# Grouped attention in one pipelined loop: the output product behind the second projection, other fixed banks, and VectorE's row of work re-ordered

## The reference, cut to what matters

```python
ln_out = _ln(hidden_states, ln_w, ln_b)
q = _ln(fp8_linear(ln_out, wq), ...)      # 8 groups x 2 heads x 128
k = _ln(fp8_linear(ln_out, wk), ...)      # 8 groups x 128
v = fp8_linear(ln_out, wv)
core = gqa(q, k, v)                       # softmax attention within the sequence
qx = _ln(fp8_linear(ln_out, wqx), ...)
kx, vx = split(cond @ w_kv_x)             # keys and values from a context
xout = gqa(qx, _ln(kx), vx)
catq = div_clamp_fp8(concat(core, xout), proj_smooth)
x = x + (catq @ wproj) * scale
```

## Time and profile before

| | |
|---|---|
| median of 3 runs | 1064.17 us (1063.57 to 1068.45) |
| the profiled execution | 1067.66 us, its span 1066.0 us |
| PE busy | 920.6 us, 86% |
| DVE busy | 728.0 us, 68% |
| ACT busy | 566.9 us, 53% |
| POOL busy | 147.2 us, 14% |
| scores of slot 4 begin | 407.89 us |
| scores of slot 32 begin | 899.07 us |

### The profile page before, as it was taken

One profiled execution on the slowest core, in us unless ns is written; L12 is line 12 of the kernel. 1 busy time (PEld: TensorE's weight loads), 2 busy tenths in 40 slices (PEclk: granted clock), 3 DMA queues, 4 the chain that ended last, 5 costly groups with the idle time before them and its releaser, 6 DMA issues. The chain is left out here.

```text
span 1066.0 us, 15923 instructions
## 1 busy us (share of the span) xinstructions
PE 920.6 (86%) x5254; PEld 691.2 (65%) x5254; DVE 728.0 (68%) x1575; ACT 566.9 (53%) x2102; POOL 147.2 (14%) x190
## 2 busy tenths in 40 slices
PE   6989896999856589999999999999999987659597
PEld 3657664566545477778787887787877775444354
DVE  4564545567774777878787888787878786446554
ACT  4351333544524577777677777777777665121131
POOL 2001202000033411121212111111111120000000
PEclk9998998999888699999999999999999998769899
DMA  6010000000100042332332423324222522200000
GB/s 203 1 59 1 0 1 1 2 1 1 41 1 20 1 114 73 89 94 68 100 80 56 124 58 101 83 58 109 71 70 55 179 57 68 49 1 1 20 0 20
DMA packets 64081, 56.77 MB, mean 53 GB/s; under 512 B 11201, under 2 KB 62978, under 8 KB 64002
## 3 DMA queue, kind: packets, MB, share of 16 engines
q1 hardware_dynamic: 63904, 55.76, 19.7%
q10 hardware_dynamic: 98, 0.03, 0.0%
HBM read 21.15 MB, written 1.05 MB: 21 GB/s over the span
## 5 line engine op out<-in xcount | busy, mean ns | idle before, releaser
L1161 ACT ACTIVATE group_probs<-ps,score_bias 128x256 f32<-128x256 f32 x256 | 117.4, 484 | 57.0 <-DVE score_bias L1496 57.0
L837 PE MATMUL ps<-group_w_hi,xq 128*128 128x256 f32 (+1 forms) x512 | 131.1, 297 | 18.8 <-POOL xq L1704 11.6
L1118 ACT ACTIVATE group_squares<-ps 128x128 f32<-128x128 f32 x384 | 103.8, 297 | 71.9 <-PE ps L837 61.7
L1496 DVE TENSOR_REDUCE score_bias<-ps 128x2 f32<-128x512 f32 x128 | 88.1, 691 | 67.8 <-PE ps L891 67.8
L837 PE MATMUL ps<-group_w_lo,xq 128*128 128x256 f32 (+1 forms) x512 | 123.9, 283 | 0.0
L878 PE MATMUL ps<-group_probsT,group_values 128*128 128x512 f32 x256 | 117.3, 602 | 2.7 <-issue 2.7
L891 PE MATMUL ps<-group_kT,group_qT 128*128 128x256 f32 x512 | 115.8, 379 | 2.3 <-ACT group_qT L1127 2.3
L891 PEld LDWEIGHTS ps<-group_kT,group_qT 128*128 128x128 f32 x512 | 97.1, 190 | 28.4 <-issue 16.8
L837 PEld LDWEIGHTS ps<-group_w_hi,xq 128*128 128x128 f32 x512 | 100.2, 196 | 21.4 <-DVE group_heads L1482 7.6
L906 PE MATMUL ps<-group_wp_hi,group_cat 128*128 128x256 f32 x256 | 71.3, 312 | 43.0 <-DVE group_cat L199 43.0
L837 PEld LDWEIGHTS ps<-group_w_lo,xq 128*128 128x128 f32 x512 | 100.6, 196 | 0.8
(11 more groups left out here) (262 smaller groups left out, 1797.9 us busy)
## 6 DMA issues: line engine op xcount, KB each, us to landing
group_probsT<-second SPq DMA_DIRECT2D x512, 64.0 KB, 2.0
group_raw_p<-in_L_xattn_wproj_dram SPq DMA_DIRECT2D x16, 256.0 KB, 3.3
group_raw_w<-in_L_xattn_wq_dram SPq DMA_DIRECT2D x8, 256.0 KB, 3.1
group_raw_w<-in_L_xattn_wqx_dram SPq DMA_DIRECT2D x8, 256.0 KB, 3.1
group_raw_w<-in_L_xattn_w_kv_x_dram SPq DMA_DIRECT2D x16, 128.0 KB, 3.2
x_all<-in_x_dram SPq DMA_DIRECT2D x2, 512.0 KB, 5.9
front_work<-in_ctx_dram SPq DMA_DIRECT2D x1, 1024.0 KB, 6.8
group_raw_w<-in_L_xattn_wk_dram SPq DMA_DIRECT2D x8, 128.0 KB, 3.0
```

What stands on the lines that cost most here:

```text
L837: last = pe.matmul(c.ps[:, bank, at:at + width], x_, w[:, k, col:col + width], start=k == 0 and m == 0, stop=k == KD - 1 and m == 1)
L1118: act.activation(c.squares[:, t, 3 * i + h, :], c.ps[:, bank, h * HD:(h + 1) * HD], ACT.Square, accum_out=c.head_sum[:, t, 3 * i + h:3 * i ...
L1161: last = act.activation(c.probs[:, side, h, t, :], c.ps[:, fills.bank(name), t * S:(t + 1) * S], ACT.Exp, bias=c.score_bias[:, i:i + 1], a ...
L1496: v.tensor_reduce(c.score_bias[:, i:i + 2], c.ps[:, bank, :].rearrange("p (t n) -> p t n", n=S), AX.X, ALU.max, negate=True).then_inc(nega ...
```

## The change

The whole diff follows. On PE the output product of item n-4 comes behind the second projection of item n. The fixed banks of the fills become a plain turn of 5, 6, 4, 7. In slot 1 two transposes of tokens go to banks 4 and 7. On DVE the first side is laid before the second side's sums are inverted and before the weights; the second side is laid before the output product is added.

```diff
-FILL_BANKS = (5, 6, 4, 7, 4, 5, 6, 7, 4, 5, 6, 7)
+FILL_BANKS = (5, 6, 4, 7, 5, 6, 4, 7, 5, 6, 4, 7)
...
     if o.weights:
         fill(WEIGHTS, WEIGHTS + 1)
-    if o.outputs:
-        fill(ADD)
     if o.projects:
         f.plan(2, ("proj", o.n, 2))
         f.plan(3, ("proj", o.n, 3))
+    if o.outputs:
+        fill(ADD)
     if o.scores:
         fill(*range(HEADS_T, HEADS_T + 3))
     if o.n == 1:
-        f.plan(5, ("xT", "Q", 1, 0))
-        f.plan(6, ("xT", "Q", 1, 1))
+        f.plan(4, ("xT", "Q", 1, 0))
+        f.plan(7, ("xT", "Q", 1, 1))
...
                     if o.weights:
                         next_weights(o)
+                    if o.projects:
+                        project_item(o, 1)
                     if o.outputs:
                         output_item(o)
-                    if o.projects:
-                        project_item(o, 1)
                     if o.scores:
                         turn_item_heads(o)
...
                     if o.outputs:
                         quantise_item(o)
                     if o.turns:
+                        lay_item_probs(o, 0)
                         invert_sums(o, 1)
                     if o.weights:
                         next_weights(o)
                     if o.turns:
-                        lay_item_probs(o, 0)
+                        lay_item_probs(o, 1)
                     if o.outputs:
                         add_item(o)
-                    if o.turns:
-                        lay_item_probs(o, 1)
                     if o.projects:
                         normalise_item(o)
```

## The result

| | before | changed |
|---|---|---|
| median | 1066.53 us, 5 runs | 1075.44 us, 5 runs |
| ratio | | 1.0086, 95% interval 1.0047 to 1.0124 |
| span of the profiled execution | 1066.0 us | 1071.8 us |
| scores of slot 4 begin | 407.89 | 407.18 |
| scores of slot 32 begin | 899.07 | 907.23 |

A forecast was written before the change was run, and what follows sets the result against it. A loop through DVE and the output product bounds the kernel; afterwards averages wait for DVE's addition. Slots 4 to 31 give +6.4 us, with start and end +5.4, so the median becomes 1069.6 us (+0.51%), range 1062 to 1076.

The forecast's parts named there:

- The loop before: Old kernel's slots: a loop of scores, DVE, output product, second projection, heads and averages sets 17.55 us, whatever PE has to do.
- The averages behind the addition: PE's averages take bank 4 behind ADD, so they wait 0.5 to 1.5 us per slot for DVE's later addition; chance 0.55.
- The lengths: New slot is 16.85 us plus weights: 18.14, 18.53, 17.86 and 16.96 for types 0 to 3, against 17.56.
- the sum: Slots 4 to 31 together +6.4 us; with start and end +5.4 us.
- Other waits: New order's waits for product, weights and reciprocal are hidden; DMAs of `probs_laid` have just enough room, so nothing is added.
- The room of 13.18: Time in us from the second side's transpose to the next first one, for 16 DMAs; one observed case took 13.05.
- The loop through `probs_laid`: Second loop, through 16 DMAs; as rival bound it needs more than 13.18 us, up to +10 us, 1080; chance 0.07.
- POOL and DVE: Second side's multiplications on DVE fall beside POOL's root of 1.3 us; price on DVE nil.
- the rival: POOL and DVE lock each other out: the root's 1.3 in each of 28 slots, 36 us, 1106; chance 0.03.
- The start: Slot 1: ACT's wait of 0.81 us for a transpose behind bank 5 goes, -0.8 us.
- so I give it no chance of its own: Rival that PE's clock falls in the new idle, waits up to 1.5 us; no separate chance given.
- The tail: Slots 32 to 35: earlier laid sides against averages waiting for the addition, taken as equal, -0.2 us, up to 2 either way.

The follow-up runs named there:

- run 114: Not a label of a run: in "In the whole run 114 multiplications" the number counts DVE multiplications beside work of POOL in the changed kernel.

## Why the prediction was right, point by point

**The loop before.** Right. In the runs in which the product moved (with new banks; it was never moved alone) and the addition wasn't late, the slots are of PE's length.

**The averages behind the addition.** Right, and shown from both sides: freeing the bank alone, and the old DVE order alone, each take the loss away. PE waits there 0.7 to 1.7 us and not 0.5 to 1.5, since the claim comes free up to 0.09 later in three of the types and PE gets there some 0.1 earlier.

**The lengths.** Forecast 18.14, 18.53, 17.86 and 16.96, measured 18.28, 18.53, 18.00 and 17.11. The terms that were off are two: the release of the claim took 0.15 (619.28 to 619.43) and not 0.05, and from the start of the averages to the scores went 3.50 (619.43 to 622.93) and not 3.44. In type 1 the weights were done in 1.55 (633.28 to 634.83 in DVE's timeline) instead of 1.68, since ACT's part had ended 1.4 earlier (at 631.92), where before the two overlapped (626.69 in the earlier trace rows, ACT's part up to 627.55); that hid both. The slots 5 to 32 grew by 8.9 (500.05 less 491.18), where the sum for the same slots was 5.8: about 0.15 more in each but type 1. The direction hung on little: 0.2 us less in each slot would have been no change, as the prediction says, and the errors of the small terms happened to lie on the slower side.

**Other waits.** Right: in the changed kernel DVE doesn't wait for DMAs between 408 and 850 us, nor the addition for the product. The room of 13.18 held; it is 13.35 in the timeline (618.71 to 632.06). The loop through `probs_laid` was rightly named as next, and the run with the addition ahead of the second side hit it.

**POOL and DVE.** Right: the second side's multiplications, 616.30 for 1.13, ran into POOL's root, which starts at 617.04 in its timeline, and were not held. In the whole run 114 multiplications lie beside work of POOL, and all took 0.34 to 0.36. By the sentence of the Trainium skill (SBUF — State Buffer, "SBUF: two separate sides") an instruction of VectorE in a two-port mode would have been held for the whole of POOL's. In which mode the multiplications run no trace shows, so they don't speak against the sentence. Another instruction shows a hold, in both kernels: a step of the rounding that makes `xq`, of the same form as the step of L196 (0.43 throughout), here in timelines of slot 1 of the kernel before.

```profile
347.78 0.43 DVE L1448 TENSOR_SCALAR front_work<-front_work 128x1024 uint16<-128x1024 uint16 x1
349.77 2.22 DVE L1448 TENSOR_SCALAR front_work<-front_work 128x1024 uint16<-128x1024 uint16 x1
```

```profile
349.48 2.23 POOL L1704 TENSOR_TENSOR xq<-front_work 128x1024 fp32r<-128x1024 bf16 x1 [6.43 <-DVE front_work L1450]
```

Of its eight executions the three without POOL took 0.43 and the five beside POOL's product 2.22. The one shown ends 0.28 behind POOL's (351.99 against 351.71), as the sentence has it. So the rival had a real ground; rows 9 settled it for the multiplications, and would not have for every instruction of VectorE.

**The start.** Here the prediction was wrong about the clock: "so I give it no chance of its own". It had the slots in mind, and there the clock did stay at 1.00. The forecast gain in slot 1 came: ACT's wait of 0.81 is gone, and from slot 1's projection to the scores of slot 2 the changed kernel is 1.2 faster. But PE's wait ahead of those scores grew from 2.29 to 3.24, both times for ACT's copies of the turned heads. In the changed kernel the first of them starts 0.47 behind the end of PE's heads (368.86 against 368.39), before it started 0.35 ahead of it. Behind the longer wait the clock was low. Timelines of PE, before and changed:

```profile
374.51 3.69 PE L891 MATMUL ps<-group_kT,group_qT 128*128 128x256 f32 x16 [2.29 <-ACT group_qT L1127]
```

```profile
371.63 6.64 PE L891 MATMUL ps<-group_kT,group_qT 128*128 128x256 f32 x16 [3.24 <-ACT group_qT L1127]
```

The same 16 matmuls took 2.95 more, and the way from these scores to the next grew by as much, from 14.32 to 17.27. In windows of PE (length, busy, clock) the changed kernel has 0.50 there, the level of 1.2 GHz, and the kernel before 1.00:

```profile
371.60:375.00 3.40, 3.37 (x8) 0.50 0.41 99
```

```profile
374.50:378.30 3.80, 3.79 (x19) 1.00 0.42 101
```

Slot 4 then was 0.8 shorter, where the sum has it 0.58 longer: before, PE had waited in it for cat (1.34) and for the addition ahead of the heads (0.84), now once, ahead of the averages, 1.64. At the scores of slot 4 the changed kernel is ahead by 0.7, but it was ahead by 1.67 already where slot 1's projection begins (327.58 against 329.25), in code that the change doesn't touch; so the start cost 1.0, where the sum up to there has a gain of 0.2 (0.8 less slot 4's 0.58). All five runs with the changed kernel's fixed banks have the wait of 3.2 and scores of 6.6 to 6.7; the banks alone are one of them, and their ratio is 1.

**The tail.** Right within 0.3, though as a balance of two effects that were only put as equal: from the scores of slot 32 to the last stage the lead of before shrinks from 8.16 to 7.73.

**From the trace to the median.** From slot 1's projection to the last stage the changed kernel takes 9.4 us more (1.0, 8.9 and -0.4), where the sum has 5.4. The spans differ by 5.8 only, since this profile was 1.7 ahead in front of it and the last stage, which is the same code, took 123.1 us instead of 125.1; it took between 123.0 and 125.1 in the ten profiles. The median's 9 us, with an interval of 5.0 to 13.2, hold the 9.4; a closer agreement isn't to be had from one profile each.

## What to carry to other kernels

When a wait is taken away by moving work, ask of each engine's order which instruction now releases the next claim: here a bank made the averages wait for an addition that had just been put last. A short release (an addition of 0.65 us that drains a shared bank) belongs ahead of work that only feeds a later slot, or its bank must go to a fill that comes later still. Changes that look like one are best taken apart: here the moved product with its banks was worth 24 us under DVE's old order, the banks alone were worth nothing under that order, and DVE's new order cost more than the first gave as long as the bank stood between them. Parts don't add up either: the same banks were worth nothing with one order of DVE and some 17 us with the other.

## What the runs showed of the hardware that I had not expected

PE's clock was at 0.50 behind a wait of 3.24 us and at 1.00 behind one of 2.29 at the same place of the program. The length of the wait alone doesn't decide, though: of the five runs with a wait of 2.28 or 2.29 there, four have scores of 3.69, and the one with DVE's order alone has 5.38.

```profile
369.73 5.38 PE L891 MATMUL ps<-group_kT,group_qT 128*128 128x256 f32 x16 [2.29 <-ACT group_qT L1127]
```

In that run the granted clock was 1.00 from 366.00 to 369.70, wait included, and 0.68 in the mean from there to 375.00. What made the difference is open. In the slots waits of 1.6 us every 18 us left the clock at 1.00.

An instruction of VectorE of 0.43 us took 2.22 where it lay beside one of GpSimd of 2.23, and four-byte multiplications beside GpSimd's root kept their time (both above).

With the product directly behind the second projection PE's own slot is 0.26 shorter than I had from the windows of before: 16.40, 17.29, 16.17 instead of 16.65, 17.55, 16.45. In the timelines the product starts 0.67 behind the start of the projection's last group (567.95 to 568.62), where the heads before started 0.86 behind it. The rest of the 0.26 stays open.
